# Early-fusion block on one core: row work moved beside the value and key units, and all three low parts of the weights on GpSimd in groups 5 to 7

## The reference

```python
h = ssm_kernel(log_dt, Lambda, x)              # (32, 128, 1024) float32
h = concatenate([h, txt], axis=1)              # txt (32, 77, 1024): 205 rows for each of 32 batch entries
h = h + attn(layernorm(h))                     # 32 query heads, 8 key/value heads, head size 32, causal
h = h + ffn(layernorm(h))                      # 1024 to 1024, base weight + Fourier-transformed low-rank update
def attn(x):
    q, k, v = x @ wq, x @ wk, x @ wv           # k and v repeated for 4 query heads each
    p = softmax(where(causal, q @ k.T * SCALE, min))
    return (p @ v) @ wo
```

## Time and profile before

| | us |
|---|---|
| median of 3 runs | 2895.55 (2894.34 to 2897.94) |
| the profiled execution's own time | 2894.3 |
| its span, first to last instruction | 2891.9 |
| PE busy | 2655.3 (92%) |
| DVE busy | 1941.2 (67%) |
| ACT busy | 1230.0 (43%) |
| POOL busy | 1144.9 (40%) |

### The profile page before, as it was taken

One profiled execution on the slowest core, in us unless ns is written; L12 is line 12 of the kernel. 1 busy time (PEld: TensorE's weight loads), 2 busy tenths in 40 slices (PEclk: granted clock), 3 DMA queues, 4 the chain that ended last, 5 costly groups with the idle time before them and its releaser, 6 DMA issues. The chain is left out here.

```text
span 2891.9 us, 70053 instructions
## 1 busy us (share of the span) xinstructions
PE 2655.3 (92%) x27456; PEld 1919.6 (66%) x27456; DVE 1941.2 (67%) x5569; ACT 1230.0 (43%) x2570; POOL 1144.9 (40%) x1810
## 2 busy tenths in 40 slices
PE   1948999999999999999999976999999999999999
PEld 1838888888888888888888952444444444444444
DVE  8966888888888888888888674644444444444443
ACT  4343676766767676766667572201000010101010
POOL 2751565656656565666656570101010101010100
PEclk9979999999999999999999976999999999999999
DMA  7756556465555555565555454454545455545553
GB/s 242 194 122 100 98 92 105 85 109 93 96 94 96 103 93 104 84 107 92 101 92 86 73 124 170 113 139 116 133 122 136 119 134 121 133 123 131 125 129 77
DMA packets 509031, 332.99 MB, mean 115 GB/s; under 512 B 421145, under 2 KB 464409, under 8 KB 508225
## 3 DMA queue, kind: packets, MB, share of 16 engines
q1 hardware_dynamic: 486192, 264.68, 46.3%
q10 hardware_dynamic: 22512, 63.84, 7.1%
HBM read 116.49 MB, written 80.61 MB: 68 GB/s over the span
## 5 line engine op out<-in xcount | busy, mean ns | idle before, releaser
L1044 PE MATMUL psJ<-xth,qh 128*128 128x205 f16 x2048 | 517.3, 253 | 51.6 <-DMA xtl<-xfl 47.6
L704 POOL TENSOR_TENSOR pl<-arena,ph 128x410 f16<-128x410 f32 (+1 forms) x512 | 501.0, 998 | 94.7 <-ACT ph L790 94.7
L1046 PE MATMUL psJ<-xth,ql 128*128 128x205 f16 x2048 | 516.3, 252 | 0.0
L1045 PE MATMUL psJ<-xtl,qh 128*128 128x205 f16 x2048 | 515.8, 252 | 0.0
L699 POOL TENSOR_SCALAR_AFFINE_SELECT arena<-arena 128x256 f32<-128x256 f32 (+1 forms) x768 | 331.7, 438 | 438.3 <-ACT arena L783 419.3
L1261 POOL TENSOR_TENSOR arena<-stage,arena 128x1024 f32<-128x1024 f32 x52 | 122.1, 2349 | 936.2 <-DVE stage L1304 936.2
L1275 ACT CAST xh<-arena 128x1024 f16<-128x1024 f32 x52 | 54.3, 1045 | 995.1 <-DVE arena L1313 995.1
L783 ACT ACTIVATE arena<-psT,escale 128x410 f32<-128x410 f32 (+1 forms) x768 | 399.6, 565 | 95.5 <-PE psT L984 57.5
L790 ACT CAST ph<-arena 128x410 f16<-128x410 f32 (+1 forms) x768 | 334.8, 500 | 14.9 <-POOL arena L699 14.7
L1304 DVE SCALAR_TENSOR_TENSOR stage<-ps5O,osc,h_in 128x512 f32<-128x512 f32 x104 | 77.9, 750 | 388.4 <-PE ps5O L1401 388.4
L885 DVE TENSOR_REDUCE mx<-psS 77x2 f32<-77x410 f32 x512 | 296.5, 579 | 60.7 <-PE psS L1031 57.0
(11 more groups left out here) (231 smaller groups left out, 6106.2 us busy)
## 6 DMA issues: line engine op xcount, KB each, us to landing
a_in<-acat SPq DMA_DIRECT2D x52, 512.0 KB, 3.8
h_in<-hcat SPq DMA_DIRECT2D x52, 512.0 KB, 4.6
qst<-qsh SPq DMA_DIRECT2D x128, 205.0 KB, 4.7
out<-stage SPq DMA_DIRECT2D x51, 512.0 KB, 3.1
hcat<-ob SPq DMA_DIRECT2D x64, 256.0 KB, 4.4
xin<-hcat ACTq DMA_DIRECT2D x32, 512.0 KB
acat<-arena ACTq DMA_DIRECT2D x64, 256.0 KB
qst<-qsl SPq DMA_DIRECT2D x64, 205.0 KB, 5.7
```

The lines of the kernel that those rows point to most:

```text
L704: pool.tensor_tensor(view(pl, g % 2, k), view(p32, g % 2, k), view(ph, g % 2, k), ALU.subtract).then_inc(lo_pool, 1)
L1044: pe.matmul(ps[:, 0:S], wh[:, k, c], xth[:, par, k, 0:S], start=k == 0, stop=False)
L1045: pe.matmul(ps[:, 0:S], wh[:, k, c], xtl[:, par, k, 0:S], start=False, stop=False)
L1046: m = pe.matmul(ps[:, 0:S], wl[:, k, c], xth[:, par, k, 0:S], start=False, stop=k == KC - 1)
```

## The change

1. `EXTRA`: the value units go to slots 1 and 2, the key units to slots 3 and 4. "m" keeps slots 0 and 4.
2. `high_part` (now for entry b+3, in the step after its statistics): pieces 0, 1 in slots 1, 2 and pieces 2 and 3 both in slot 3, each after the copies of the slot's units. `low_part`: pieces 0, 1 in slots 2, 3, pieces 2 and 3 in slot 4. The statistics stay in slots 1 to 3.
3. In groups 5, 6 and 7 POOL makes all three parts of `pl`, and DVE none.
4. The loads of `xin` and the stores of the result move from ACT's queue to SP's. ACT's copy of the values is one instruction in slot 1 and one in slot 2, after the high parts and no longer ahead of the exponentials.
5. SP's order in a step: the value transposes come first, then `turn(0)`, the restacks, `turn(1)`, the shift of the maxima, store, load. The thirteen small loads for the next block go out one in each step from b = 1, no longer all in step 30. `wo` is loaded at the end of step 29.
6. Start: the peaks are complete two chunks earlier. SP loads entry 0 alone and entry 1 behind it. For entry 0 DVE does the refinement rounds itself, its high and low parts come ahead of or between the low parts of the weights, and its transposes are issued piece by piece.

The core of the diff:

```diff
-        EXTRA = {0: ("v", 0), 1: ("v", 1), 2: ("k", 0), 3: ("k", 1)}
+        ALL_POOL = (5, 6, 7)
+        EXTRA = {1: ("v", 0), 2: ("v", 1), 3: ("k", 0), 4: ("k", 1)}
+        HIGH, LOW, LINK = {1: (0,), 2: (1,), 3: (2, 3)}, {2: (0,), 3: (1,), 4: (2, 3)}, {1: 0, 2: 1, 3: 2}
...  GpSimd
-                    for k in (1, 2):
+                    for k in (0, 1, 2) if g in ALL_POOL else (1, 2):
-                    if g == 3 and has["ln"]:
+                    if g == 4 and has["ln"]:
                         scale_rows(b)
...  ScalarE
-                    if g == 3 and has["load"]:
-                        act.wait_ge(x_lo, 4 * (b + 4))
-                        load(b + 5, 1 - par)
-                    if g == 2 and has["last"]:
-                        store(b - 1, 1)
-                    if g == 2 and has["max"]:
-                        values(b + 1)
-                    if g == 6 and has["att"]:
-                        store(b, 0)
+                    if g in (1, 2) and has["max"]:
+                        values(b + 1, g - 1)
-                    if g >= 4 and has["ln"]:
-                        high_part(b, par, g - 4)
+                    if has["turn"] and b > -3:
+                        for piece in HIGH.get(g, ()):
+                            high_part(b + 3, piece)
...  VectorE
+                    if b == -4:
+                        rsqrt_rounds(link, dve, rs[:, b % 2])
-                    if has["att"]:
+                    if has["att"] and g not in ALL_POOL:
+                    if b == -3 and g == 0:
+                        for part, ks in (((0, 1), (4, 5)), ((2, 3), (6, 7))):
+                            for piece in part:
+                                low_part(0, piece)
+                            weights_low(0, ks)
+                        weights_low(1, range(KC))
+                    if has["turn"] and b > -3:
+                        for piece in LOW.get(g, ()):
+                            low_part(b + 3, piece)
...  SyncE, at the end of a step
+                if has["load"]:
+                    sp.wait_ge(x_lo, 4 * (b + 4))
+                    load(b + 5, 1 - par)
+                if 1 <= b < len(ahead):
+                    dst, src, arrived = ahead[b]
+                    sp.dma_start(dst, src).then_inc(arrived, 16)
```

More of the change, by code:

```diff
@@ L598, in step @@
                     shift_rows(1, par)
[L599 to L604, removed]
+                if has["last"]:
+                    store(b - 1, 1)
+                if has["qkv"]:
+                    wait(sp, pj_lo, base + at(rows, "v", 1) + 1)
+                    wait(sp, v_ok, 2 * (b + 2))
+                    if b == -2:
+                        sp.wait_ge(values_ok, 1)
+                    for c in range(2):
+                        for k in range(2):
+                            sp.dma_start_transpose(out=vt[:, k, :, c * P:(c + 1) * P], in_=vst[k][:, c, :]).then_inc(v_in[c], 16)
                 if has["turn"]:
@@ L608, in step @@
                     turn(0, nxt, b + 3)
-                    turn(1, nxt, b + 3)
                 if has["qkv"]:
@@ L616, in step @@
                     restack(Q_PARTS, qst[par][:, 0], HALVES[0], q_in[0])
[L617 to L622, removed]
+                if has["turn"]:
+                    turn(1, nxt, b + 3)
                 if has["max"]:
@@ L712, in _, with high_part, values @@
         def _(act):
[L713 to L723, removed]
+            def high_part(m, n):
                 t, h = divmod(n, 2)
                 c, r = slice(h * D // 2, (h + 1) * D // 2), T[t]
-                x = xin[0:r, par, t, c]
+                x = xin[0:r, m % 2, t, c]
                 if n == 0:
-                    act.wait_ge(ln_done, b + 5)
+                    act.wait_ge(ln_done, m + 1)
                 if h == 0:
[L731 to L736, removed]
+                    wait(act, xt_in[t], 32 * m)
+                act.activation(x, x, ACT.Identity, bias=nmean[0:r, m % 2, t:t + 1]).then_inc(centred, 1)
+                act.wait_ge(centred, 4 * m + n + 1)
+                act.activation(xfh[0:r, t, c], x, ACT.Copy, scale=rs[0:r, m % 2, 3, t:t + 1]).then_inc(x_hi, 1)
+            def values(n, k):
                 for q in v_in:
@@ L759, in step @@
                 if b == -3:
+                    for n in range(4):
+                        high_part(0, n)
+                    n = 0
                     weights_high(1)
@@ L814, in _, with weights_low @@
             dve.wait_ge(cleared, 1)
-            def weights_low(n):
-                for k in range(KC):
+            def weights_low(n, ks):
+                for k in ks:
                     dve.wait_ge(w_hi, n * KC + k + 1)
@@ L939, in step @@
                         take_maxes(b, j, base, (0, 1), late_read)
[L940 to L945, removed]
-                            weights_low(0)
-                        for piece in {6: (0,), 7: (1, 2)}.get(g, ()):
-                            low_part(b + 4, piece)
-                        if b == -3 and g == 0:
-                            weights_low(1)
+                    if b == -3 and g == 0:
[7 more added lines that the diff above has]
+                            low_part(b + 3, piece)
+                    if has["ln"] and g in LINK:
+                        layer_norm(b, par, LINK[g])
+                    if b == -4 and g == NKV - 1:
+                        weights_low(0, range(4))
                     if has["att"] and g:
```

77 lines of the change are left out of this document (51 added, 26 removed).

## The result

The changed kernel took 2910.89 us, median of 7 runs (2904.99 to 2922.25); the kernel before took 2897.69 beside it. Their ratio is 1.0045, 95% interval [1.0028, 1.0063]: slower by 13 us. The forecast was 2885.5. The time lies just above the upper end of the range, 2908, and on the other side of no change.

A forecast was written before the change was run, and what follows sets the result against it. PE, 92% busy, bounds the kernel; only its waits can be won. Start -8, steps -1, step 28 +1.3, step 29 -0.7, end -1.7 sum to -10 us: median 2885.5 us, range 2866 to 2908.

The forecast's parts named there:

- slot 4's term for VectorE: Slot 4: two low parts delay the query unit's split that frees the PSUM bank for "m"; 0.35 us, between 0 and 1.3.
- The second rival: VectorE in slot 4 makes PE wait and the slot grows by 1.3 us: +26 us, about 2912 us; chance 0.12.
- The other slot terms: Added PE time per step: slot 0 0.14 us, slot 1 0.2, slots 2 and 3 0.58 each, slots 5 to 7 nothing.
- the wait for ScalarE covers VectorE's lateness: VectorE ends slots 2 and 3 about 1.2 us late, covered by PE's wait for ScalarE in the next slot.
- The start: Before step 0: PE starts 12.4 us earlier, partly lost to later stalls; -8 us, bounds -13 and -2.
- Step 28: Row pieces for the last entry now run in this step: +1.3 us.
- step 29: This step loses slot 2's and most of slot 0's loss: -0.7 us.
- The end: Steps 30 and 31: the 4.1 us wait for the shift goes, GpSimd adds 2.4 us in slots 5 to 7; -1.7 us.
- Row work is hidden after all: Rival: ScalarE's idle time hides row work; PE's steps 43.3 us, 27 x -3.2, about 2800 us; chance 0.08.

The follow-up runs named there:

- early_split: Against early: VectorE's row low part moved behind the query split in slots 2 to 4 and behind the norm in slot 5; 2824.65 us.
- split_first: Changed kernel with VectorE's two row low parts of slot 4 placed behind the query unit's split; 2882.32 us.
- early: Changed kernel with one ScalarE piece in each of slots 1 to 4, ahead of the value or key unit's copy, low parts in slots 2 to 5; 2814.89 us.
- start_load: Changed kernel with SyncE's order before step 0 changed: first rows, restacks, shift, second rows, next rows' load, value transposes last; 2900.38 us.
- dve_pl: Changed kernel with its GpSimd half undone: VectorE again makes the first low part of the weights in groups 5 to 7; 2908.00 us.
- best: Changed kernel with early's ScalarE pieces, low parts behind the query split in slots 2 to 4 and ahead in slot 5, and start_load's order; 2787.11 us.
- low_spread: Changed kernel with VectorE's low part of row piece 3 moved from slot 4 to slot 5; 2885.48 us.
- best_dve_pl: Against best: VectorE again makes the first low part of the weights in groups 5 to 7, GpSimd two of three; 2813.01 us.
- start_sp: Changed kernel with SyncE's order before step 0 changed: first rows, restacks, shift, second rows, value transposes, load; 2906.71 us.

## Why the prediction was wrong, step by step

- **What failed: slot 4's term for VectorE.** The step says: "In slot 4 two low parts push the split of the query unit behind the place at which PE wants its PSUM bank for "m": between 0 us (both at 0.74) and 1.3 us (both at 1.5 and the norm late); I take 0.35." The mechanism is right, the size isn't: it measures 9.41 - 8.49 = 0.92 us. That is 0.57 us per step too little, 15 of the 25 us by which the forecast missed. With small misses in the other slots the step is 0.66 us over the sum, 17.8 us over 27. The choice was made between the ends, though the text itself says a little further on that all four low parts keep their long time. The trace now shows 1.493 and 1.252 us for the two (medians of steps 2 to 26). The "median" of 1352 ns in the earlier trace rows was no guide either: before, the four low parts of a step took 1.253, 1.495, 0.741 and 1.451 us in every step, so 1.352 is a value between two of them that none took.
- The second rival, with its chance of 0.12, named this mechanism. Its number, about 2912 us, is close partly by luck: it had the step at +1.0 us, measured +0.62, and the start's whole gain of 8 us, which didn't come.
- The paragraph behind that sentence leans on the Trainium skill, page "SBUF — State Buffer", section "Who interferes with whom": a VectorE instruction with two SBUF inputs contends with a GpSimd instruction that reads SBUF. Here the runs agree: 1.49 us beside the subtraction, 0.74 with it cut to 16 columns. The rule was right and was left out of the number. One by one, the four instructions in slot 4 of step 14, GpSimd's first:

```profile
974.53 0.96 POOL L746 TENSOR_TENSOR pl<-arena,ph 128x410 f16<-128x410 f32 x1 [0.38 <-ACT ph L815]
974.55 1.49 DVE L896 SCALAR_TENSOR_TENSOR xfl<-xin,rs,xfh 77x512 f16<-77x512 f32 x1
975.46 1.21 POOL L746 TENSOR_TENSOR pl<-arena,ph 77x308 f16<-77x308 f32 x1
975.97 1.25 DVE L896 SCALAR_TENSOR_TENSOR xfl<-xin,rs,xfh 77x512 f16<-77x512 f32 x1
```

  With none of the other's beside them, a low part takes 0.74 us (early_split, slots 2 and 3), a subtraction of 128x410 0.96 and one of 77x308 0.77 (split_first, slot 4). So the first low part is stretched here, then the second subtraction, then the second low part: the rows fit two engines that take turns by whole instructions. Both low parts end 0.55 us behind the end of the subtraction in front of them, which is how a moved low part could have been priced.
- The other slot terms held in size: slot 0 4.56 (forecast 4.55), slot 1 6.55, slot 2 6.94 and slot 3 6.99 (6.93), slots 5 to 7 4.24 (4.25). Slot 2's 0.6 us went with the piece (early, 6.35). Slot 3's did not: there the size was right by luck and the cause wrong. The prediction says that the wait for ScalarE covers VectorE's lateness; in slot 3 PE has no wait for ScalarE, and 0.45 us for VectorE's query split. The slot fell to 6.36 only when the low part went behind the split.
- **The start: -2.7 us instead of -8.** Most of the chain was right: statistics 188.75 (forecast 191), PE's first matmul 209.03 (211.5), the fourth unit 223.54 (225.2), the next step's first matmul 246.54 (246.9), though its row names a restack where the forecast had a transpose. What the forecast left out is the clock and the shift. PE waits 3.58 us for that restack, and its granted clock in 246 to 253 us is 0.52 (between the two levels, nearly all at 1.2 GHz), where the kernel before was granted 1.00 from 232 us on. Half the speed for 6.8 us costs 3.4. Then step 0 waits 2.47 us for the shift, issued at 281.41 as the last of sixteen transfers without a pause. PE's timeline:

```profile
246.54 0.61 PE L1060 MATMUL psS<-kst,qst 96*128 96x128 f16 x4 [3.58 <-DMA qst<-qsl]
...
284.08 0.52 PE L1017 MATMUL psT<-qst,kst 98*128 98x410 f16 x2 [2.47 <-DMA qst<-ml]
```

  start_load removes both waits and gains 8.5 us at step 0's start. And -2.7 is a good execution: in the nine profiled versions with SyncE's order of the changed kernel step 0 starts between 283.70 and 289.05 us, with a median of 286.39, against 286.76 before. Six of them, the two with the same code among them, have a wait of 3.1 us for a split at the fourth unit, where this execution has 1.52. This fits the median of the seven runs, which lies 5.9 us above the profiled execution, where the forecast took 1.25; why the split comes later in some executions stays open.
- Step 0, in which all of slot 4's cost already falls, was in no term: +1.2 us. Step 28 +2.0 (forecast 1.3), step 29 -0.9 (-0.7).
- **The end: -5.6 us instead of -1.7.** The wait for the shift is gone as forecast. Most of the rest goes with the clock: in step 30 PE was granted 0.92 on average, before 0.71, and its busy time for the same 403 matmuls fell from 24.90 to 21.35 us. I had no term for it. That the higher clock followed from the removed wait is only argued; versions without that wait got 0.64 (dve_pl) and 0.69 (best) as well, so what sets it in this step stays open. Step 31 took 1.6 us more, where the forecast had +2.4 for GpSimd over both steps.
- "Row work is hidden after all" was given 0.08 for this change, rightly: it isn't. But the price named for it, about 2800 us, is near what the best version reached (2787) once the pieces stood ahead of the unit's copy.

## What to carry to other kernels

Work moved "beside" a long wait fills it only if it stands ahead of the instruction that waits, in its engine's own order; behind it, the same work lands on the next critical instruction. When a row shows several durations for one instruction, find what runs beside it at each, and price the moved one by its new neighbour, not by a median over all. And a wait that another covers isn't gone: price it again each time the cover is removed, as with slot 3's split and with `pl` in groups 5 to 7.

## What the runs showed of the hardware

- A VectorE low part with two SBUF inputs, 77x512, takes 0.74 us with nothing of GpSimd's beside it, and 1.49 or 1.25 beside GpSimd's subtractions in slot 4 of the changed kernel. GpSimd pays too: in slot 3 it was busy 3.46 us with the overlap (early) and 3.04 without it (best), for the same five instructions.
- The long low parts follow the end of GpSimd's subtraction: in steps 2 to 26 of before, after, low_spread, early, early_split and best_dve_pl, all 375 low parts of more than 1.1 us end 0.54 to 0.55 us behind the end of the subtraction that was running when they began.
- An overlap alone doesn't say which of the two is stretched. In slot 7 of step 14 of the kernel before, a low part ran beside a subtraction at its short 0.74 us, and the subtraction, which had begun 0.37 us earlier, took 1.93 instead of 0.96:

```profile
982.66 0.74 DVE L862 SCALAR_TENSOR_TENSOR xfl<-xin,rs,xfh 128x512 f16<-128x512 f32 x1
982.29 1.93 POOL L704 TENSOR_TENSOR pl<-arena,ph 128x410 f16<-128x410 f32 x1 [0.38 <-ACT ph L790]
```

  Beside GpSimd's affine selections the low part took 0.74 us in low_spread and early and 0.94 in best, and the three selections 1.71, 1.69 and 1.67 us, against 1.42 in slot 4 of the changed kernel.
- The second low part in a row in that slot is as repeatable as the first: 1.251 to 1.253 us over 25 steps. Such collisions are a fixed pattern of the order, not noise.
- A wait of PE of 3.58 us was followed by 6.8 us at half the clock in step -1, and in the nine versions with this wait (3.2 to 4.0 us) the granted clock of the 7 us behind it was 0.56 to 0.78. The 29 waits of 1.65 and 0.76 us in the steps left it at 1.00. The length of the wait alone doesn't decide: in start_sp a wait of 2.69 us at 254.58 left 1.00 over the next 7 us, and one of 2.55 at 292.44 was followed by 0.76.
